# One exponential of 1024 columns over two PSUM banks in place of two of 512 columns, in a state-space scan on one core

## The reference, cut to what matters

```python
dt = jnp.clip(jax.nn.softplus(xc @ dt_W + dt_b), DT_MIN, DT_MAX)
A = -jnp.exp(A_log)                       # N = 64 values
def step(h, ins):                         # h: (8 batches, E = 256 channels, N = 64 states)
    x_t, dt_t, B_t, C_t = ins
    dA = jnp.exp(dt_t[..., None] * A)
    h = dA * h + dt_t[..., None] * B_t[:, None, :] * x_t[..., None]
    y_t = jnp.einsum('ben,bn->be', h, C_t)
    return (h, y_t)
```

## Time and profile before

| | us |
|---|---|
| runs (3) | 1293.88, 1300.1, 1325.05 |
| median | 1300.1 |
| the profiled execution, its own time | 1294.7 |
| span of the profile, first to last instruction | 1292.7 |
| busy in the span: PE / DVE / ACT / POOL | 1152.1 / 1050.2 / 1041.8 / 861.5 |

### The profile page before, as it was taken

One profiled execution on the slowest core, in us unless ns is written; L12 is line 12 of the kernel. 1 busy time (PEld: TensorE's weight loads), 2 busy tenths in 40 slices (PEclk: granted clock), 3 DMA queues, 4 the chain that ended last, 5 costly groups with the idle time before them and its releaser, 6 DMA issues.

```text
span 1292.7 us, 34025 instructions
## 1 busy us (share of the span) xinstructions
PE 1152.1 (89%) x10152; PEld 514.8 (40%) x10152; DVE 1050.2 (81%) x2254; ACT 1041.8 (81%) x1748; POOL 861.5 (67%) x1220
## 2 busy tenths in 40 slices
PE   4999973888999999999999999999999999898998
PEld 2666651223343334343433343434343434343435
DVE  3578773878888888888888888888888888888884
ACT  1666663879888888888888888888888888888891
POOL 5355443767777777777777767676767676777771
PEclk9898975769999999999999999999999999999999
DMA  4022334111111111111111111111111111111100
GB/s 122 33 102 100 102 120 130 44 27 30 32 35 33 32 35 33 32 32 31 33 33 33 33 33 33 33 33 33 33 33 33 33 33 33 33 33 33 34 6 9
DMA packets 73848, 56.50 MB, mean 44 GB/s; under 512 B 43968, under 2 KB 63296, under 8 KB 70720
## 3 DMA queue, kind: packets, MB, share of 16 engines
q1 hardware_dynamic: 73792, 55.80, 14.5%
HBM read 36.38 MB, written 19.40 MB: 43 GB/s over the span
## 4 chain that ended last, share of the span: by engine, by line
PE 45%; DVE 16%; issue 10%; ACT 4%; POOL 4%; DVEq 1%; ACTq 0%; POOLq 0%
PE ps L961 14%; PE ps L867 9%; PE ps L873 7%; PE ps L1056 7%; DVE state L1156 6%; DVE ps L1147 5%; PE ps L1070 4%; POOL decayed L812 3%; ACT state L1109 2%; PE ps L1021 2%; DVE c_cols L1192 2%; DVE n L1255 1%; DVE y_tok L1201 1%; PE ps L1034 1%; ACT square L1124 1%
## 5 line engine op out<-in xcount | busy, mean ns | idle before, releaser
L812 POOL TENSOR_TENSOR decayed<-decay,state 128x256 f32<-128x256 f32 x1024 | 727.4, 731 | 279.7 <-DVE state L1156 259.2
L1097 ACT ACTIVATE decay<-ps,a_col 128x512 f32<-128x512 f32 x1024 | 704.8, 693 | 100.1 <-PE ps L867 67.1
L1147 DVE TENSOR_TENSOR ps<-decay,ps 128x512 f32<-128x512 f32 x512 | 354.7, 693 | 111.9 <-ACT state L1109 81.1
L867 PE MATMUL ps<-moving,dt_pick 48*128 48x256 bf16 x2048 | 404.4, 279 | 30.7 <-DVE state L1156 20.9
L1156 DVE TENSOR_TENSOR state<-decayed,ps 128x256 f32<-128x256 f32 x1024 | 392.4, 416 | 28.7 <-POOL decayed L812 10.0
L961 PE MATMUL ps<-state,c_cols 128*32 128x256 f32 x4096 | 335.1, 400 | 0.0
L1109 ACT COPY state<-ps 128x512 f32<-128x512 f32 x512 | 297.4, 581 | 32.8 <-DVE ps L1147 30.5
L873 PE MATMUL ps<-moving,b_rows 48*128 48x256 bf16 x1024 | 201.7, 278 | 66.2 <-DVE ps L1147 65.0
L867 PEld LDWEIGHTS ps<-moving,dt_pick 48*128 48x128 bf16 x2048 | 115.3, 94 | 244.9 <-issue 219.5
L880 PE MATMUL ps<-moving,b_rows 48*128 48x256 bf16 x1024 | 203.4, 279 | 0.0
L1056 PE MATMUL ps<-h,w 128*128 128x256 f32 x512 | 172.4, 422 | 1.0 <-DVE h L1281 0.8
(11 more groups left out here) (122 smaller groups left out, 1004.1 us busy)
## 6 DMA issues: line engine op xcount, KB each, us to landing
moving<-u_stage SPq DMA_DIRECT2D x64, 288.0 KB
moving<-dt_stage SPq DMA_DIRECT2D x64, 96.0 KB
b_stage<-b_parts SPq DMA_DIRECT2D x24, 192.0 KB, 2.7
b_rows<-b_stage SPq DMA_DIRECT2D x256, 18.0 KB
dt_stage<-dt_parts SPq DMA_DIRECT2D x8, 512.0 KB, 2.8
u_stage<-u_parts SPq DMA_DIRECT2D x8, 512.0 KB, 3.2
dt_stage<-dt_parts SPq DMA_DIRECT2D x8, 256.0 KB, 2.1
u_stage<-u_parts SPq DMA_DIRECT2D x8, 256.0 KB, 2.4
```

The source lines that it names most:

```text
L812: nc.gpsimd.tensor_tensor(decayed[:, p], decay[:, k % RING, p * E:(p + 1) * E], state[:, (k - 1) % RING, p * E:(p + 1) * E], ALU.mult).the ...
L867: return nc.tensor.matmul(ps[:, DTP + f, p * E:(p + 1) * E], dt_pick[rows(f), p, :], moving[rows(f), cb, kk, :], start=True, stop=True)
L1097: nc.scalar.activation(decay[:, k % RING, f * SELF:(f + 1) * SELF], ps[:, DTP + f, :], ACT.Exp, scale=a_col[:, 2:3]).then_inc(ready, 1)
L1147: nc.vector.tensor_tensor(ps[:, ACCP + k % 2, :], decay[:, k % RING, SELF:QE], ps[:, ACCP + (k - 1) % 2, :], ALU.mult).then_inc(acc_decaye ...
```

## The change

The two exponentials of a step become one instruction of 1024 columns that reads both banks `DTP` and `DTP + 1` and writes both halves of `decay`. The two semaphores `self_decay_ready` and `acc_decay_ready` become one, `decay_ready`, which is raised once, when the 1024 columns are done. Every wait for either of the two now waits for that one: POOL's for the self half, DVE's for the acc half, and PE's ahead of the self picks and ahead of the acc picks. ACT now waits for both sets of picks, and for both readers of the ring's slot, ahead of the one instruction.

```diff
--- before.py
+++ after.py
@@ -705,8 +705,7 @@
 
             self_dt_spread = sem("self_dt_spread")
             acc_dt_spread = sem("acc_dt_spread")
-            self_decay_ready = sem("self_decay_ready")
-            acc_decay_ready = sem("acc_decay_ready")
+            decay_ready = sem("decay_ready")
             self_decayed = [sem(f"self_decayed{p}") for p in range(Q // 2)]
             acc_decayed = sem("acc_decayed")
             self_input = sem("self_input")
@@ -804,7 +803,7 @@
                     def decay_self(i, k):
 
                         t = i * STEPS + k
-                        wait_step(pool, self_decay_ready, t)
+                        wait_step(pool, decay_ready, t)
                         if known(t) and t == 0:
                             pool.wait_ge(start_zeroed, 1)
                         for p in range(Q // 2):
@@ -913,7 +912,7 @@
                         spreads = not (known(t) and t + 2 >= T)
                         if spreads:
                             wait_moving(i, k + 2)
-                            wait_step(pe, self_decay_ready, t + 1)
+                            wait_step(pe, decay_ready, t + 1)
                         wait_step(pe, acc_decayed, t)
                         for p in range(HQ):
                             acc = acc_matmul(i, k, p)
@@ -930,7 +929,7 @@
                         spreads = not (known(t) and t + 2 >= T)
                         multiplies = not (known(t) and t + 1 >= T)
                         if spreads:
-                            wait_step(pe, acc_decay_ready, t + 1)
+                            wait_step(pe, decay_ready, t + 1)
                         if multiplies:
                             wait_b(i, k + 1)
                             wait_step(pe, self_state[1], t)
@@ -968,8 +967,8 @@
                         t = i * STEPS + k
                         if known(t) and t == 0:
                             for first in range(2):
-                                spread_first(0, first, self_dt_spread, self_decay_ready)
-                                spread_first(1, first, acc_dt_spread, acc_decay_ready)
+                                spread_first(0, first, self_dt_spread, decay_ready)
+                                spread_first(1, first, acc_dt_spread, decay_ready)
                             self_first()
                         add_acc_and_spread_self(i, k)
                         if k % TC == LAG:
@@ -1090,12 +1089,13 @@
                         t = i * STEPS + k
                         if known(t) and t >= T:
                             return
-                        for f, spread, ready, used in ((0, self_dt_spread, self_decay_ready, self_decayed[1]),
-                                                       (1, acc_dt_spread, acc_decay_ready, acc_decayed)):
-                            wait_step(act, spread, t)
-                            wait_step(act, used, t - RING)
-                            nc.scalar.activation(decay[:, k % RING, f * SELF:(f + 1) * SELF], ps[:, DTP + f, :],
-                                                 ACT.Exp, scale=a_col[:, 2:3]).then_inc(ready, 1)
+                        wait_step(act, self_dt_spread, t)
+                        wait_step(act, acc_dt_spread, t)
+                        wait_step(act, self_decayed[1], t - RING)
+                        wait_step(act, acc_decayed, t - RING)
+                        nc.scalar.activation(decay[:, k % RING, :],
+                                             ps[:, DTP:DTP + 2, :].rearrange("p f e -> p (f e)"),
+                                             ACT.Exp, scale=a_col[:, 2:3]).then_inc(decay_ready, 1)
 
                     def copy_state(i, k):
                         t = i * STEPS + k
@@ -1140,7 +1140,7 @@
 
                     def step(i, k):
                         t = i * STEPS + k
-                        wait_step(dve, acc_decay_ready, t)
+                        wait_step(dve, decay_ready, t)
 
                         dve.wait_ge(acc_state, t + 1)
                         wait_step(dve, acc_copied, t - 2)
```

## The result

The changed kernel takes 1674.6 us (median of 4 runs, 1656.58 to 1686.88); the kernel before, run beside it, takes 1312.57. The ratio is 1.2865, 95% interval [1.2653, 1.3078]: slower by some 29%. Ratios here are of fast runs alone: a run over 1.5% above the fastest of its kernel is left out of them. The profiled execution took 1656.6 us, 361.9 more than the profiled one of before.

A forecast was written before the change was run, and what follows sets the result against it. PE was busiest but no engine full, so the answer lay inside one scan step. To the profiled 1294.7 us it added 40 for the first body and 461 for the other 480 steps: 1795 us, range 1600 to 1980.

The forecast's parts named there:

- The loop: Scan step: PE's acc matmuls to acc picks and ACT's exponential alternate without overlap, 2.49 us at full clock against 2.04.
- PE's piece: On PE, from acc matmul to end of acc picks: 1.28 us of each step at full clock.
- What was counted as hidden: PE's finishing work (0.63 us), ACT's copy (0.58), POOL's multiplies and add (1.88) and DVE's multiply would not lengthen the step.
- One sign: Trace mark of being right: line 1097 first among PE's waits, some 1.2 us a step.
- The clock: PE's granted clock falls in each body's light half and rises in its heavy half; mean step 3.00 us.
- a moved one: The one step in 16 with acc picks ahead of the contraction: 1.92 us at full clock, some 2.8 at half.
- the 16 light ones: Steps of each body with about half the heavy finishing work, PE busy 0.64, all counted at half clock.
- so many short waits were enough: Before the old kernel's clock fell, PE waited for DVE ten times, 5.1 us in all, never over 1.1.
- The clock that stays up: Rival: PE's clock stays up past the first body, 1532 us; chance 0.17.
- The clock that hardly rises: Rival: PE's clock hardly rises again after falling, 1954 us; chance 0.20.
- The gain on ACT: Rival: ACT ends the step, one 1.12 us instruction replaces a 1.27 us pair, 1218 us; chance 0.03.
- The two banks in one instruction: Rival: ACT's merged exponential starts the second bank anew, 1.38 us, adding 133 us to whichever case holds; no separate chance.

The follow-up runs named there:

- e1: Changed kernel with its 1024-column exponential split into two of 512, merged waits kept: 1878.57 us, ratio 1.4387.
- e2: Changed kernel with PE's acc picks and self matmuls ahead of the contraction in every step: 1323.76 us, ratio 1.0161.
- e4: Changed kernel with the acc half's exponential left out, DVE using the self half, all waits and picks kept: 1372.87 us, ratio 1.0531.
- e8: Changed kernel with one 256-column matmul of zeros on PE in step 13 and in the first body's steps: 1562.28 us, ratio 1.2084.
- e10: Kernel before with a 128-column matmul of zeros on PE in the first body's steps: 1320.47 us, ratio 1.0174.

## Why the prediction came out as it did

*The loop* was right. Both turns, the order of waits and their size hold: 1.28 us of PE's piece, the instruction 1.12 (1.116 on average), the time from its end to PE's start 0.06. The time from the end of the picks to ACT's start was 0.08, not 0.03, so the step is 2.54 us, not 2.49, and its mean at full clock 2.50, not 2.45. e1, e2 and e4 move this step as the terms say. At half clock it is 3.41, not 3.37.

*What was counted as hidden* stayed hidden: finishing work, ACT's copy, POOL's and DVE's pieces. PE waited for DVE's lines 1147 and 1156 for 2.0 us in all. One sign was not met as written: PE stood 0.61 us a step for the exponential, not some 1.2, since its finishing work fills the rest.

*The clock* was right in kind and mis-sized. The first body's 3.33 was 3.25. In the other bodies the mean was to be 3.00 us from 20 of 32 steps at half clock; it was 2.72, which is (2.72 - 2.50)/(3.39 - 2.50) = 0.25, or 8 of 32 (3.39 is 15 steps of 3.41 and a moved one of 3.1, which was to be 2.8). The difference, 480 x 0.28 = 134 us, is nearly the whole miss from 1796 to 1657. The term that was mis-sized is the number of steps at half clock, and the step behind it that failed is "the 16 light ones". There are no sixteen. I had taken K_H2's two records of 256 columns for two matmuls and set them against one instruction of the other steps; a 4-byte matmul shows as two records, so those others hold two as well, like the 0.70 us of line 1020 above. The trace of before already had the row, right behind those of the earlier trace rows:

```profile
704.96 0.70 PE L1021 MATMUL ps<-xn_feat,w 128*128 128x256 f32 x2
```

The description of the finishing work ahead of the prediction has the same error, and so has that of the contraction: its "eight matmuls" are four, with eight records. PE's finishing work is nearly even: 0.66 to 0.71 us at full clock in 26 of the 32 steps, 0.87 to 1.13 in five, and none in step 13. In 13 of the last 14 bodies the clock was down from step 14 to step 18; ten of these falls began at step 13 or 14, three at step 10 or 11, and they lasted 17 to 31 us. Four short falls, of 3.4 to 10.2 us, began at other steps. e8 shows that filling step 13 keeps the clock up; what brought it down where no step was empty stays open.

That the number fell inside the range is in part luck. The profiled 1656.6 us lies 138 us under the forecast and 125 above the first rival's 1532, and fewer steps ran at half clock than the range allowed: its fewest, 10 of 32, stood for 1664 us. The time is inside because the low end also takes off 51 us for a shorter instruction, which did not come. What tells the two apart is the trace: a clock of 0.83 from the first to the last multiply and 0.50 in the first body.

The Trainium skill says in TensorE: Matmul & The Clock Gate, section "A second HAM failure mode: psum-queue depth-cycling", that frequent small idles make the clock swing. The trace agrees in part: seven of the 17 falls came behind waits of 0.76 us at most. But e8 had such waits too, 422 of them and none over 0.8 us, and its clock stayed at 1.00 for 1132.4 us. So the prediction's "so many short waits were enough" fits those seven falls and not e8.

*The rivals.* The clock that stays up (1532 us) was not it; e8 comes near it, once the empty step is filled. The clock that hardly rises was not it. The gain on ACT exists, 0.15 us an instruction by e1, but ACT idles 0.95 us in each step, so it buys nothing. The two banks in one instruction cost nothing extra: 1.116 us, where 1.38 was feared.

## What to carry to other kernels

Merging two instructions of an engine merges their waits. If the two stood at different points of a loop between engines, the later start and the later end of both now count for each, and a saving of 0.15 us on the engine turned into 0.50 us on the step. Ask first whether the buffer they share with the producer is single; if it is, either keep them apart or, as e2_order did, reorder the producer so that all inputs come first and its other work lies under the merged instruction. A second pair of banks was not tried. And compare an engine's work from step to step by the busy time that the trace shows, not by counting records in one step and matmuls in another.

## What was not expected of the hardware

- The share of time that PE was busy did not tell when the granted clock would rise. In the changed kernel it rose after stretches of 17.1 us with PE busy 98%; in e10 it stayed at 0.50 through 91.8 us at 98%, in e8 through 58.0 us at 90%.
- Ten of the changed kernel's 17 falls of the clock came at its one step in 32 without finishing work or the next, and lasted 17.1 or 20.5 us each. With 44 small matmuls of zeros, in that step and the first body, the kernel took 112 us less.
- The same short waits, none over 0.8 us, stood ahead of seven falls in the changed kernel and of none in 1132.4 us of e8.
- A matmul of 4-byte operands has two records in the profile (1016 for 508); a transpose of 4-byte operands on PE has one (64 for the 64 of line 996 in the kernel before).
